# A cross-attention key loop on one core, reordered from sixteen heads to eight slots of two heads

## The reference

```python
x = x + xattn(layernorm(x), ctx)        # ctx: 12544 x 512
# in xattn, for the 257 image rows and for the 12287 text rows apart:
q = rms_norm(q_in @ q_w.T + q_b) * norm_q_w          # 128 x 16 heads x 32
k = rms_norm(c @ k_w.T + k_b) * norm_k_w
v = c @ v_w.T + v_b
out += softmax(q @ k.T / sqrt(32), axis=keys) @ v    # by head
x = x + self_attention(layernorm(x))
x = x + experts(layernorm(x))
```

## Time and profile before

| what | value |
|---|---|
| time, three runs | 1211.66, 1211.16, 1208.44 us; median 1211.16 |
| span of the profiled execution | 1210.0 us (its own time isn't listed apart from the three) |
| PE busy | 1172.7 us, 97% |
| DVE busy | 979.3 us, 81% |
| ACT busy | 853.0 us, 70% |
| POOL busy | 763.8 us, 63% |
| granted clock of TensorE, mean | 0.990 |
| scores of group 0 begin | 57.2 us |
| last transposes of the output | 973.9 us |

### The profile page before, as it was taken

How to read it: one execution, slowest core, us unless ns; L and a number is a source line. 1 busy time by engine, 2 the same in 40 slices (tenths; PEclk the granted TensorE clock), 3 DMA queues, 4 the chain that set the end, 5 groups by cost and what they waited for, 6 DMA issues and landing times.

```text
span 1210.0 us, 26425 instructions
## 1 busy us (share of the span) xinstructions
PE 1172.7 (97%) x8794; PEld 940.5 (78%) x8794; DVE 979.3 (81%) x1657; ACT 853.0 (70%) x1845; POOL 763.8 (63%) x1064
## 2 busy tenths in 40 slices
PE   6999999999999999999999999999999779899998
PEld 4768888888888888888888888888887558588886
DVE  4768888878888888888888887888877779499997
ACT  5567777777767777777777777677777757378885
POOL 7987888888888878788887888888873100000000
PEclk9999999999999999999999999999999989999999
DMA  7135686665776667756668666686653899469990
GB/s 253 41 97 154 164 218 168 172 171 151 212 177 176 166 168 186 207 155 175 171 168 215 168 175 163 154 218 171 175 135 97 257 394 397 190 253 366 360 365 21
DMA packets 132400, 236.74 MB, mean 196 GB/s; under 512 B 18086, under 2 KB 45222, under 8 KB 131884
## 3 DMA queue, kind: packets, MB, share of 16 engines
q1 hardware_dynamic: 132268, 235.06, 66.4%
HBM read 140.87 MB, written 17.04 MB: 130 GB/s over the span
## 4 chain that ended last, share of the span: by engine, by line
PE 89%; POOL 5%; DVE 2%; issue 1%; ACT 1%; DMA 1%; SPq 0%; POOLq 0%; DVEq 0%; ACTq 0%
PE ps L1500 36%; PE ps L1363 18%; PE ps L1526 9%; PE ps L1570 8%; PE ps L1694 3%; PE ps L1697 3%; PE ps L1700 3%; PE ps L1715 1%; PE ps L1723 1%; PE ps L1719 1%; PE ps L1671 1%; PE ps L1610 1%; PE ps L1614 1%; PE ps L1607 1%; POOL cx_blocks L613 1%
## 5 line engine op out<-in xcount | busy, mean ns | idle before, releaser
L1500 PE MATMUL ps<-w_text,cx_blocks 128*128 128x512 f32 x1974 | 536.7, 397 | 1.3 <-ACT v_first L803 0.7
L1500 PEld LDWEIGHTS ps<-w_text,cx_blocks 128*128 128x128 f32 x1974 | 366.4, 189 | 65.8 <-issue 2.7
L846 ACT ACTIVATE p<-ps,small 128x512 f32<-128x512 f32 (+2 forms) x400 | 271.1, 678 | 203.1 <-DVE small L1167 199.7
L1165 DVE TENSOR_REDUCE small<-ps 128x1 f32<-128x512 f32 (+2 forms) x400 | 270.6, 677 | 110.2 <-PE ps L1526 109.9
L1363 PE MATMUL ps<-ident,p 128*128 128x128 f32 x1584 | 239.8, 273 | 8.8 <-DVE pt L1158 7.0
L1363 PEld LDWEIGHTS ps<-ident,p 128*128 128x128 f32 x1584 | 193.9, 140 | 63.9 <-issue 12.4
L1526 PE MATMUL ps<-k_stack,q_stack 96*128 96x512 f32 (+1 forms) x400 | 191.9, 480 | 1.2 <-ACT p L846 1.2
L828 ACT ACTIVATE pt<-ps 128x512 f32<-128x512 f32 (+1 forms) x250 | 147.6, 591 | 12.3 <-PE ps L1363 8.0
L615 POOL TENSOR_TENSOR cx_blocks<-cx_sum,cx_blocks 128x256 fp32r<-128x256 f32 x188 | 139.3, 741 | 14.8
L613 POOL TENSOR_TENSOR cx_blocks<-cx_sum,small 128x256 fp32r<-128x256 f32 x188 | 118.2, 629 | 44.8 <-PE ps L1500 37.0
L1167 DVE TENSOR_TENSOR small<-small 128x1 f32<-128x1 f32 x400 | 132.4, 331 | 13.7
(11 more groups left out here) (252 smaller groups left out, 1935.2 us busy)
## 6 DMA issues: line engine op xcount, KB each, us to landing
expert<-experts SPq DMA_DIRECT2D x34, 1536.0 KB, 8.7
k_stack<-kt_hi SPq DMA_DIRECT2D x384, 128.0 KB, 2.5
cx<-ctx_t SPq DMA_DIRECT2D x48, 512.0 KB, 4.4
k_stack<-kt_lo SPq DMA_DIRECT2D x192, 128.0 KB, 2.5
codes<-codes SPq DMA_DIRECT2D x64, 256.0 KB, 4.5
code_scale<-code_scales SPq DMA_DIRECT2D x256, 64.0 KB, 4.0
scaled<-codes SPq DMA_DIRECT2D x64, 256.0 KB, 4.4
weight_q<-scaled SPq DMA_DIRECT2D x1, 4096.0 KB, 15.6
```

The lines of the kernel that those rows point to most:

```text
L846: eng.activation(pb[:, lo:hi], score_bank(s, h)[:, lo:hi], exp, bias=nm[1 - par][:, h:h + 1], accum_out=ls[1 - par][:, h:h + 1]).then_inc( ...
L1165: eng.tensor_reduce(ngm[:, h:h + 1], score_bank(s, h)[:, lo:hi], AX.X, ALU.max, negate=True).then_inc(e_gm, 1)
L1500: last = eng.matmul(ps_a[(p + i + 1) % 2][:, :], blk[:, i, a, c * P:(c + 1) * P], w_t[:, i, w, c * D:(c + 1) * D], start=(i in FRESH and c ...
```

## The change

The loop over 16 heads becomes a loop over 8 slots `j`, each with heads `2j` and `2j + 1`. A slot of TensorE is now: the transposes of both heads of the slot before, a key tile's transposes (slots 2 to 5) or the output's (slot 6), both scores, in slots 1 and 5 two value batches, and then one run of products (12, 6, 12 and 12 in the four slots of a half). ScalarE and VectorE follow the same slots. VectorE copies heads 2, 3, 10 and 11 only. In the last steps (`draining`) the old order by heads stays. On GpSimd `key_norm` moves ahead of a split at two places. The sync queue's program is unchanged.

```diff
-        PROD = ((0, 7, 14, 21, 23, 28, 35, 40, NPROD), (0, 7, 12, 19, 21, 26, 33, 40, NPROD))
-        KT_SLOTS, KT_AFTER = (4, 6, 7, 9), (2, 2, 2, 3)
-        KT_HIGH, KT_LOW = (5, 6, 7, 9), (5, 6, 8, 9)
-        BY_DVE = (0, 1, 7, 8, 10, 15)
+        SLOTS = NH // 2
+        PROD = (0, 12, 18, 30, NPROD)
+        PV_AT, KT_AT, OT_AT = (1, 5), (2, 3, 4, 5), 6
+        SQUARE_AT, SCALE_AT = {0: 1, 1: 2, 4: 3}, {1: 1, 2: 2, 4: 3}
+        BY_DVE, BY_DVE_LAST = (2, 3, 10, 11), (0, 1, 7, 8, 10, 15)
...
+                if cur:
+                    key_norm(s, 3, 1)
                 if strass:
                     split(0, 6, quarter(0, 1, 1), 0)
-                if cur:
-                    key_norm(s, 3, 1)
...
+                if g or j:
+                    eng.wait_ge(e_sq, g * GT + j)
                 eng.activation(squares[:, :], kb[KB_OF[j]][:, :], square, scale=D ** -0.5,
```

ScalarE's slot:

```diff
+                def slot(j):
...
+                    if more and kk == 2:
+                        store_product(p, 2)
+                    if cur and j == 1:
+                        square_keys(s, SQUARE_AT[j], 1)
+                    if nxt and j == 5:
+                        square_keys(s + 1, 0, 1)
+                    for h in (2 * j, 2 * j + 1):
+                        store(h, 2)
+                    if end and j == 2:
+                        store_attention()
+                    if cur and j in (0, 4):
+                        square_keys(s, SQUARE_AT[j], 1)
+                    if cur and j in KT_AT:
+                        if j == KT_AT[0]:
+                            stacked_last()
+                        keys_high(s, KT_AT.index(j), 1)
+                    if score:
+                        exponential(2 * j)
+                    if more and kk == 2:
+                        store_product(p, 3)
+                    if score:
+                        exponential(2 * j + 1)
+                    if cur and j in SCALE_AT:
+                        scale_keys(s, SCALE_AT[j], 1)
+                    if nxt and j == 6:
+                        scale_keys(s + 1, 0, 1)
```

VectorE's slot:

```diff
+                def slot(j):
...
+                    if cur and j == 0 and s > 1:
+                        second_key_tile(s - 1, 0)
+                    if cur and j == 4:
+                        second_key_tile(s, -1)
+                    if more and kk == 1:
+                        first_key_tile(p)
+                    if more and kk == 3:
+                        values(p, 1)
+                    for h in (2 * j, 2 * j + 1):
+                        store(h, 2)
                     if score:
+                        maximum(2 * j)
+                        maximum(2 * j + 1)
+                    if cur and j in KT_AT:
+                        keys_low(s, KT_AT.index(j), 1)
+                    if more and kk == 0:
+                        first_key_tile_started(p)
+                    if more and kk == 3:
+                        values(p, 0)
+                    if end and j == 5:
+                        scale_attention()
+                    if end and j == OT_AT:
+                        add_attention()
```

TensorE's slot:

```diff
+                def slot(j):
...
+                    for h in (2 * j, 2 * j + 1):
+                        transpose_probabilities(h, 2)
+                    if cur and j in KT_AT:
+                        transpose_keys(KT_AT.index(j))
+                    if end and j == OT_AT:
+                        transpose_attention()
+                    if score:
+                        products_of_queries(2 * j)
+                        products_of_queries(2 * j + 1)
+                    if j in PV_AT and (score if j == PV_AT[1] else end):
+                        for c in range(NH // HC // 2):
+                            weigh_values(*behind(g, 2 * j, 7 - HC * c))
+                    if nxt if p == 0 else cur:
+                        products_of_pair(p, kk)
```

More of the change, by code:

```diff
@@ L894, in step @@
+                    if s >= NG or h > 9:
                         store(h, 2)
-                    if nxt and h == 10:
-                        square_keys(s + 1, 0, 1)
-                    if nxt and h == 14:
-                        scale_keys(s + 1, 0, 1)
+                for j in range(SLOTS):
+                    if draining(s, 2 * j):
+                        drain(2 * j)
+                        drain(2 * j + 1)
+                    else:
+                        slot(j)
                 if score:
@@ L1193, in step, with drain @@
+                def drain(h):
+                    if cur and h == 8:
+                        second_key_tile(s, -1)
+                        keys_low(s, 2, 1)
+                    if score:
+                        maximum(h)
+                    if cur and h == 10:
+                        keys_low(s, 3, 1)
+                    store(h, 4)
                     if s == NG - 1 and h == 8:
@@ L1229, in _ @@
+                    if end and h == 14:
+                        add_attention()
+                for j in range(SLOTS):
+                    if draining(s, 2 * j):
+                        drain(2 * j)
+                        drain(2 * j + 1)
+                    else:
+                        slot(j)
             steps(eng, step)
@@ L1527, in products_of_queries, with transpose_probabilities @@
                                          start=True, stop=True).then_inc(e_qk, 1)
-                for h in range(NH // 2 if (not loop and s == 0) else 0, NH):
+                def transpose_probabilities(h, lag):
+                    gp, hp = behind(g, h, lag)
+                    if score if gp == g else end:
+                        eng.wait_ge(e_exp, gp * NH + hp + 1)
+                        if gp > 0 or hp >= 2:
+                            go, ho = behind(gp, hp, 2)
+                            dve = stored_by_dve(go, ho)
+                            eng.wait_ge(e_pte if dve else e_pta, stored(dve, go, ho))
+                        transposes(ps_pt[hp % 2], p_sb[hp % NP], IT if gp == 0 else GT).then_inc(e_pt, 1)
```

309 lines of the change are left out of this document (139 added, 170 removed).

## The result

The changed kernel takes **1236.12 us** (median of four runs, 1232.28 to 1247.65) against 1211.41 for the kernel before beside it (1208.44 to 1212.89): ratio 1.022 (of the means; the medians stand 24.7 us apart, 2.0%), 95% interval 1.018 to 1.026. It is about 2% slower. The forecast was 1212, with 1200 to 1227 as the range, so the time lies outside it.

The account below looks back on a forecast made before the run. TensorE's own stream was taken to bound the kernel. Stream 36.46, slots 5 and 6 0.60 and spread of V 0.30 made 37.36 us a step against 37.33, some +1 us: 1212, range 1200 to 1227.

Parts of the forecast that it names:

- The stream: TensorE's work in a key-loop step if nothing waits: 36.46 us, 0.87 less than 37.33, 19 us over 22 steps.
- A pair of value batches: On TensorE in slots 1 and 5: two batches in a row cost 2.11 us against 2.42 as single ones.
- The stacking DMAs: Rival, chance 0.20: ScalarE's key tile 0 copy in slot 2 waits for the sync queue's DMAs; step 37.7 us, time 1220.
- the main sum: Whole step: 36.46 + 0.60 + 0.30 = 37.36 us against 37.33, some +1 us in all; chance 0.32.
- Slots 5 and 6: TensorE waits for exponentials: 0.09 and 0.24 us lost from slot 5's copies, 0.26 in slot 6, together 0.6 a step.
- The spread of V: V, the time of VectorE's 128x1 operation, varies: 0.30 us a step lost over slots 0, 3, 4, 7 (bounds 0 and 0.96).
- What was put at nothing: Costs taken as free: GpSimd's swapped splits, two copies a step moved to ScalarE, a square's wait, the drain's order.
- rival 1: The pairs' chains fit under TensorE's stream, V near 0.16: step 36.9 us, time 1202; chance 0.30.

Follow-up runs that it names:

- experiment 3: Changed kernel without the low parts' stacking DMAs from group 2 on (eight of 24 a step; scores stale): 1223.96 us, ratio 1.009.
- experiment 5: Kernel of experiment 3 with ScalarE's high part of key tile 3 copied ahead of slot 5's two head copies: 1211.52 us, ratio 0.999.
- experiment 6: Kernel of experiment 5 with GpSimd's second code scaling moved behind the split of product 5: 1197.88 us, ratio 0.989.
- experiment 12: Kernel of experiment 10 with two of its four ScalarE-issued DMAs back on the sync queue and VectorE's output scaling moved from slot 5 to 6: 1217.84 us.
- experiment 4: Changed kernel with the third code tile passed behind the second stack of DMAs and GpSimd's code scalings later: 1266.76 us, ratio 1.046.
- experiment 9: Kernel before with eight more stacking DMAs a step, into partitions that nothing reads: 1314.43 us, ratio 1.087.
- experiment 10: Changed kernel, all stacking kept, key tile 3 copied earlier, second code scaling later, four stacking DMAs issued by ScalarE: 1204.91 us, ratio 0.995.
- experiment 2: Changed kernel with the four DMAs that load a code tile's scales made one DMA of the same 128 rows: 1287.39 us, ratio 1.057.

## Why the prediction was wrong

- **The stream** was right: 36.46 us forecast, 36.3 from the shortest slots of experiment 3. A pair of value batches takes 2.00 us (score at 518.51, products at 521.05, less 0.54 for two scores), forecast 2.11.
- **The stacking DMAs** are the step that failed. It had the place, the copy of tile 0 in slot 2, and the shape, a loop. But it stood as a rival with a chance of 0.20 and a step of 37.7, and the main sum went on as if it cost nothing. Its own bounds were 16.5 + 20.4 to 22.2 = 36.9 to 38.7. The step of the changed kernel has 16.74 + 21.94 + 0.03 = 38.71: the upper end. I had taken 21.2 for the DMAs, near the middle of the bounds. Issues of 0.64 alone give the lower one; the upper one has long issues in both stacks, and that is how it is: 27 issues in the 18 steps take 1.6 us in the mean, 1.0 more than the rest, and the earlier trace rows had one of 1.24 in plain sight. A loop that may be longer than the sum can't be added at a fifth of its weight: the step is the longer of the two, and 38.7 against 37.36 was not close. At 38.7 the rival is 1211 + 22 x 1.37 = 1241, which the range up to 1227 left out.
- **Slots 5 and 6** were in part right. Slot 5 was put at 0.33 and costs 0.42 (0.41 in the changed kernel); experiment 5 took it away with the edit that the argument pointed at. Slot 6 was put at 0.26 and costs 0.57 in experiment 3 and 0.23 in experiment 6, but not for the reason given (experiment 12).
- **The spread of V** was treated as chance, 0.30 over four slots. With the loop gone it is not: the mean was near (366 ns in experiment 3) and the place was missed. GpSimd's order is fixed, its code scaling of 1.29 us met the small operation of head 7 in each step, and that one slot lost 0.62 us. Experiment 6 showed it. In the changed kernel itself the mean was right (348 ns), the meeting comes and goes with the codes, and the slot lost 0.25; that this is near the 0.30 is luck.
- **What was put at nothing**: the codes. The queue is later in each step, and GpSimd's wait for them rose from 0.6 to 30.8 us. Experiments 4 and 9 show that this wait turns into late key norms once it grows; how much of the changed kernel's own 1.4 us it holds was not separated.

Of the 24.7 us, then: without the DMA loop the time is 1224, so the loop is 12 (15 by the ratios), and what the chains cost beyond the gain of TensorE's stream is the other 12. These shares hold for taking the loop away first; with it there, some 1.3 us of a step stand at the loop's place and 1.1 in the chains (0.48, 0.41 and 0.25), since slot 3 loses less. With the loop gone and two places of the chains mended (experiment 6) the new order stands at 1197.88, 13.6 us under the kernel before; rival 1 had 1202, and the stream alone 22 x 0.87 = 19 us. So the gain on TensorE was there, and was lost at a few places. The kernels of experiments 3, 5 and 6 leave out work that the result needs; the fastest that does all of it (experiment 10) is at 1204.91.

## What to carry to other kernels

When a reordering spreads a producer over more slots, close every ring that runs through it and a DMA queue, and compare the ring's length with the step's: the longer one is the step, and slack that the old order had doesn't show in any list of waits. Count a queue's time by its issues, the long ones included, and look at what else the queue carries: in experiment 2 the DMAs behind one slow load landed late too. Two instructions of which one waits for the other can meet at the same place in every step of a static order, so ask which two meet rather than take the mean of their durations, and look whether they still meet in the kernel that you change.

## What the runs showed of the hardware

- A broadcast load of 256 KB as one DMA (experiment 2) was used 9.3 us after its issue, four of 64 KB landed 3.8 us after theirs. The last stacking DMA of 128 KB issued behind it landed after 5.2 us in the mean in place of 2.5.
- A stacking DMA's issue on the sync queue takes 0.59 to 0.60 us and the next follows 0.64 after it; of all issues there 27 of 776 took 1.1 to 2.2 us (26 of 815, 0.9 to 1.7, in the kernel before). On ScalarE it takes 0.62 us in the median, beside running activations (experiment 10).
- VectorE's operation on 128x1 elements took 0.16 to 1.32 us; in the changed kernel each of the 109 over 0.3 us ended within 0.1 us of the end of a GpSimd operation.
